# A graph network on one core: three groups of edge types asked for ahead of three bases and W1, and the maxima, scales and base splits at later slots

## The reference, cut to what matters

```python
# x: 1250 x 512, 40000 edges (src, dst sorted, type of 32, weight), bases: 8 x 512 x 512
h = relu(layernorm(x))
weight = einsum('rb,bio->rio', w_comp, bases)          # 32 relations from 8 bases
h_rel = einsum('ni,rio->rno', h, weight)
x = x + segment_sum(h_rel[type, src] * edge_weight, dst) + h_bias
h = relu(layernorm(x))
# second layer: graph convolution with self loops
u = h @ W1.T + b1
x = x + relu(segment_sum(norm[:, None] * u[row], col)) # norm = rsqrt(deg[row]) * rsqrt(deg[col])
```

## Time and profile before

| what | value |
|---|---|
| time, median of 3 runs | 731.87 us (731.0 to 733.36) |
| profiled execution, first to last instruction (its span) | 625.8 us |
| profiled execution, whole time | not given by the page |
| PE busy | 496.4 us, 79% of the span |
| DVE busy | 328.6 us, 52% |
| POOL busy | 352.2 us, 56% |
| ACT busy | 151.9 us, 24% |
| mean granted TensorE clock | 0.905 of full speed |

### The profile page before, as it was taken

How to read it: one execution, slowest core, us unless ns; L and a number is a source line. 1 busy time by engine, 2 the same in 40 slices (tenths; PEclk the granted TensorE clock), 3 DMA queues, 4 the chain that set the end, 5 groups by cost and what they waited for, 6 DMA issues and landing times.

```text
span 625.8 us, 15841 instructions
## 1 busy us (share of the span) xinstructions
PE 496.4 (79%) x5824; PEld 317.0 (51%) x5824; DVE 328.6 (52%) x929; ACT 151.9 (24%) x272; POOL 352.2 (56%) x473
## 2 busy tenths in 40 slices
PE   3031445598999899999999998999897876889996
PEld 1020334356666556666656665566564554545443
DVE  7898038885665446636655556645542221544121
ACT  3392234532222122211322202203210000341021
POOL 3334536786676776766747757677677777200000
PEclk9665657599999999999999999999997977789999
DMA  9896965557786887886858868778788788323042
GB/s 283 306 362 216 391 161 150 166 152 211 217 278 202 255 259 205 256 262 175 272 153 252 258 189 262 222 235 273 210 250 261 216 234 240 118 68 102 2 98 68
DMA packets 53427, 132.82 MB, mean 212 GB/s; under 512 B 12173, under 2 KB 18174, under 8 KB 53350
## 3 DMA queue, kind: packets, MB, share of 16 engines
q0 software_dynamic: 27040, 99.60, 53.1%
q1 hardware_dynamic: 25356, 30.99, 15.9%
q10 hardware_dynamic: 954, 1.13, 0.6%
HBM read 120.58 MB, written 11.10 MB: 210 GB/s over the span
## 4 chain that ended last, share of the span: by engine, by line
PE 52%; DMA 14%; DVE 12%; issue 8%; ACT 5%; POOL 5%; SPq 3%; ACTq 1%; POOLq 0%; DVEq 0%
PE PS L1521 22%; PE PS L1501 16%; DMA gath<-rows_layer,srcs 9%; PE PS L1595 7%; POOL gath L722 5%; PE PS L1541 4%; DMA types<-types_by_slot 2%; SPq L579 2%; DVE room_b L1225 2%; ACT room_b L841 2%; DVE zt L1225 1%; DMA edge_records<-room_c 1%; DVE room_b L1261 1%; DMA w1t<-edge_records,w1t 1%; PE PS L1507 1%
## 5 line engine op out<-in xcount | busy, mean ns | idle before, releaser
L722 POOL DMA_INDIRECT gath<-rows_layer,srcs x335 | 335.7, 1002 | 165.1 <-issue 84.8
L1501 PE MATMUL PS<-sel,gath 128*128 128x48 f16 (+7 forms) x4020 | 299.1, 207 | 52.8 <-DMA gath<-rows_layer,srcs 21.8
L1501 PEld LDWEIGHTS PS<-sel,gath 128*128 128x128 f16 x4020 | 235.4, 103 | 163.9 <-issue 86.6
L1521 PE MATMUL PS<-room_b,zt 128*128 128x512 f16 x480 | 168.6, 392 | 1.5 <-DVE sel L1147 1.0
L1521 PE MATMUL PS<-room_b 128*128 128x512 f16 (+1 forms) x480 | 151.7, 384 | 2.0 <-DMA gath<-rows_layer,srcs 1.8
L1141 DVE TENSOR_TENSOR masks<-iota_n,dloc 128x24 bf16<-128x24 f32 (+12 forms) x92 | 17.9, 194 | 96.6 <-issue 58.8
L1507 PE MATMUL PS<-oh_ad,gath 128*128 128x30 bf16 (+7 forms) x335 | 65.1, 194 | 0.0
L782 ACT CAST val<-val_f 128x64 f16<-128x64 f32 x42 | 11.0, 262 | 201.8 <-DVE val_f L1098 196.8
L1521 PEld LDWEIGHTS PS<-room_b 128*128 128x128 f16 (+1 forms) x480 | 47.8, 105 | 16.8 <-DMA gath<-rows_layer,srcs 2.1
L1521 PEld LDWEIGHTS PS<-room_b,zt 128*128 128x128 f16 x480 | 45.2, 100 | 8.6 <-issue 2.2
L1147 DVE TENSOR_TENSOR sel<-masks,val 128x192 f32<-128x192 bf16 (+12 forms) x92 | 38.6, 420 | 0.0
(11 more groups left out here) (202 smaller groups left out, 409.9 us busy)
## 6 DMA issues: line engine op xcount, KB each, us to landing
room_b<-in_L_gnn_bases_dram SPq DMA_DIRECT2D x8, 1024.0 KB, 9.3
gath<-rows_layer,srcs POOLq DMA_INDIRECT x335
types<-types_by_slot SPq DMA_DIRECT2D x168, 16.0 KB
x_t<-x_base SPq DMA_DIRECT2D x19, 128.0 KB
u_t<-in_x_dram SPq DMA_DIRECT2D x9, 256.0 KB, 6.2
x_base<-u_t SPq DMA_DIRECT2D x9, 256.0 KB
x_layer<-x_t SPq DMA_DIRECT2D x18, 128.0 KB
u_t<-x_layer SPq DMA_DIRECT2D x18, 128.0 KB, 2.7
```

Of the source, the lines that this page charges most:

```text
L722: pool.indirect_dma_start(out=gath[:, s % UN, :], out_offset=None, in_=tab0_d[:, :], in_offset=bass.IndirectOffsetOnAxis(ap=srcs[:, s:s + ...
L1501: mm(there, gath[:, s % UN, D * t + P * f:D * t + P * (f + 1)], sel_parts[:, here, k, 0:NB * w, u], start=first and t == 0 and u == 1, sto ...
L1521: last = mm(PS[0:r, PBANK[q], :], zt[q % 2][:, t, f, b, 0:r], base_hl[:, b, u, f, :], start=(m == 0), stop=(m == NM - 1))
```

## The change

Two lists are changed. SP asks for the types of groups 3, 4 and 5 together with groups 1 and 2, ahead of bases 5 to 7, the biases and W1. In the written order, "largest" moves from step 7 to 15 and "scale" from 8 to 16, and base n is split in step 17 + 2n instead of 10 + 3n, so in 17 to 31. The squares of bases 5 to 7 and of W1 stay in steps 0 to 3. Within a step, "largest" stands behind the own column of tile 0, and in step 27 the own column of tile 1 ahead of the split of base 5.

```diff
@@ -258,12 +258,12 @@
-        SQ_SETUP, SC_AT, BS_AT, WT_AT = BEARLY, 7, 10, 38
+        SQ_SETUP, SC_AT, BS_AT, WT_AT = BEARLY, 15, 17, 38
         for r in range(NTI):
             STEPS[LAST[r]].append(("flush", r))
             STEPS[LAST[r] + (3 if r + 1 < NTI else 1)].append(("own", r))
         for n in range(NB):
-            STEPS[BS_AT + 3 * n].append(("bsplit", n))
+            STEPS[BS_AT + 2 * n].append(("bsplit", n))
@@ -593,7 +593,7 @@
-            for v in range(1, TRING):
+            for v in range(1, TRING + VEARLY):
                 load_types(v)
             for n in range(BEARLY, NB):
                 load_base(n)
@@ -625,8 +625,6 @@
             sp.wait_ge(s_tab0, 16 * (NT + 3))
             sp.dma_start(w_in, W1.rearrange("(c p) i -> p c i", p=P)).then_inc(s_win, 16)
             sp.wait_ge(s_xbase, 16 * NT)
-            for v in range(TRING, TRING + VEARLY):
-                load_types(v)
             load_x(0)
             load_x(1)
```

## The result

The changed kernel took 736.2 us (median of 20 runs), the kernel before 732.3 us in the runs beside it; the ratio of the fast runs is 1.007, 95% interval 1.0049 to 1.0091, so about +5.1 us (the medians of all runs differ by 3.9). The forecast was 737.0 us, +5.2. The sign, the size and the likeliest case hold.

The account below looks back on a forecast made before the run. PE bounds the kernel from slot 38, which hangs on the last base split. W1's landing +6.5 and DVE's order -1.3 gave +5.2 on 731.87: 737.0 us, range 733.5 to 740.5, wide range 731.5 to 741.5.

Parts of the forecast that it names:

- likeliest case: Whole kernel: slower than before, 737.0 us (+5.2), chance of being slower 0.68.
- Types and the stop at slot 7: SP's queue: types land near 62 us at the latest, PE's 13.4 us stop goes, bases go out at 59.8.
- What is late next: PE stops after slot 12, ending near 77.5 us, for flush 0 behind ACT's square of W1; about 17 us.
- T: W1's landing, when ACT's square of it starts: from 83.56 to 90.1 us (87.8 to 92.3), +6.5, with 21 gathers issued before.
- The estimate that was hung on it: DMA engines: with exactly even turns between queues, T would be about 1 us earlier and the sum 1 us less.
- The order on DVE: DVE from W1's landing T: scales at T+15.2, last split ends at T+50.3 against T+51.6, so -1.3 us.
- From the last split to slot 38: Slot 38 hangs on the last split and moves with it; slot 37 just inside, costing nothing, at most +0.5.
- From slot 38 to the end: From slot 38 on PE is the bound, so a shift of slot 38 should reach the end whole.
- gathers give way: DMA: SP's queue runs at base 5's rate, W1 lands at 78.4, below 82.7 deciding; 725.4 us, chance 0.12.
- No change: DMA bill small: fewer gathers out, T near 86, sum +1.1, 733 us; chance 0.20.
- The change doesn't act: SP stuck in a types wait, DVE still waiting at group 3; chance 0.02, within the 0.20 of no change.
- The aim without ACT's hold: Slots 7 to 15 run before W1's landing T, scales at T+6.9, 729.3 us; within the 0.12.

Follow-up runs that it names:

- e4: The changed kernel with ACT's square of W1 moved from step 3 to step 15; ratio 0.9953 to the kernel before.
- e9: The changed kernel run again, unaltered, in a group where the kernel before takes 627.9 us; ratio 1.0136 to the kernel before, +8.5 us.
- e0_before: The kernel before, unchanged, profiled on a 732 us chip as neighbour of the changed kernel's profile; ratio 0.9974, span 730.6 us.
- e3: The changed kernel with POOL held before the gather of slot 15 until W1 is squared; ratio 1.0078 to the kernel before.
- e1: The kernel before with only the types of groups 3 to 5 moved ahead of the bases, steps left; ratio 1.0083 to the kernel before.
- e5: The changed kernel with types of groups 3 to 5 asked for behind bases 5 to 7, ahead of biases and W1; ratio 0.9959 to the kernel before.
- e10: The kernel before with DVE's half of the last base split done three times, same values; ratio 1.0074 to the kernel before, +4.7 us.
- e8: The changed kernel with types of groups 3 to 5 behind bases 5 to 7, W1 ahead of biases, its square in step 15; ratio 0.9972 to the kernel before.
- e11: The same kernel as e8, run again in another group; ratio 0.9927 to the kernel before.
- e2: The kernel before with only largest, scale and splits moved to the new steps, types left behind W1; ratio 1.0032 to the kernel before.

## Why the prediction was right, and where it was not

**Types and the stop at slot 7**: right. Twenty issues take 10.29 us, 0.51 each where 0.46 was taken, so the bases go out at 60.88, not 59.8. The 13.4 us wait is gone.

**What is late next**: right, in place and nearly in size. PE stops behind slot 12 (15.9 us, "about 17" was said) because ACT's square of W1 stands ahead of the cast and flush 0. The three ACT rows at 91.72, 93.63 and 93.76 show it and e4 proves it: with the square moved, slot 13 ends 10 us earlier. Slot 12 ended at 81.0, not 77.5 (78.3 in e9); 2.2 us of that are four stops inside slots 9 and 11 of the unnamed kind told of under e0_before, which e9 doesn't have.

**T**: the direction and the causes right, the size too small. 91.72 where 90.1 (87.8 to 92.3) was taken, +7.7 against e0_before, not +6.5; and in e9 93.41, past that range, +9.9 against the 83.56 that the prediction started from. The bases went out 1.1 us later than taken, which may be part of it. POOL shows the 21 gathers; the last of them and the first that had to wait:

```profile
84.74 0.95 POOL L720 DMA_INDIRECT gath<-rows_layer,srcs  x1 [1.05 <-remote]
...
99.45 1.18 POOL L720 DMA_INDIRECT gath<-rows_layer,srcs  x1 [13.77 <-PE PS L1505]
```

The two parts of the step: without the six gathers T came 4.2 us earlier (e3), and what is left, 3.6, is the head start (e1: 87.29 - 83.99 = 3.3, with one gather more than before). They aren't separate prices, though. With the head start kept (e5, on another chip), five more gathers went with a T only 1.9 us later; 1.9 and 3.6 make 5.5, so some 2 us of the 7.7 seem to come only when both are there. The queues from 60 to 78 us, answering to the earlier trace rows:

```profile
q1 hardware_dynamic: 1722, 3.16, 49.3%
q0 software_dynamic: 837, 3.08, 48.0%
```

Between them 6.24 MB in 18 us, less than the 6.94 of before. The difference lies in the first 4 us, when the bases asked for at 60.88 had hardly begun to come: 0.94 MB against 1.52. From 64 to 78 us it is 5.36 against 5.48 MB. The same rows in e9:

```profile
q0 software_dynamic: 924, 3.42, 53.8%
q1 hardware_dynamic: 1472, 2.76, 43.6%
```

There the gathers took the larger share, the last of the 21 was issued at 79.71 and not at 84.74, and W1 came 1.7 us later. The Trainium skill (DMA: Bandwidth & Descriptors, Queues, rings and completion order) says that an engine takes turns between its queues packet by packet. The shares of 49.3 and 48.0% are even, those of e9 (43.6 and 53.8%) are not, and by the profile's count SP's queue moved twice as many packets as the gathers (1722 to 837), so these rows neither show such turns nor exclude them. The estimate that was hung on it, T 1 us earlier, did not come.

**The order on DVE**: right. Scales at T+14.8 (T+15.2 was said), last split at T+49.7 (T+50.3), in the changed kernel and again in e5 (T+14.8, T+49.7) and e9 (T+49.8), whose T differ by 7.5 us. Slot 37 lies inside the splits: 138.4 against 141.4. To the last split the shift against e0_before is 7.7 - 1.8 = 5.9 us, where 6.5 - 1.3 = 5.2 was forecast.

**From the last split to slot 38**: here a term was left out. The step said that slot 38 hangs on the last split and moves with it. It moved by 8.0, not 5.9. PE around it in the changed kernel, then in e0_before:

```profile
138.24 0.18 PE L1505 MATMUL PS<-oh_ad,gath 128*128 128x50 bf16 x1
142.38 2.72 PE L1519 MATMUL PS<-room_b,zt 128*128 128x512 f16 x6 [3.96 <-DVE sel L1145]
144.90 0.45 PE L1499 MATMUL PS<-sel,gath 128*128 128x88 f16 x3
145.13 1.06 PE L1519 MATMUL PS<-room_b,zt 128*128 128x512 f16 x2
```

```profile
136.49 1.46 PE L1521 MATMUL PS<-room_b,zt 128*128 128x512 f16 x6
138.26 0.30 PE L1501 MATMUL PS<-sel,gath 128*128 128x88 f16 x3 [0.32 <-DVE room_b L1225]
138.40 0.60 PE L1521 MATMUL PS<-room_b,zt 128*128 128x512 f16 x2
```

And the changed kernel's windows there (length, busy of PE, weight loads, DVE, ACT and POOL, PE clock, DMA share, GB/s):

```profile
138.00:140.00 2.00, 0.43 (x8) 0.18 (x4) 0.96 (x1) 1.00 (x1) 1.39 (x3) 1.00 0.61 179
140.00:142.00 2.00, 0.00 (x0) 0.00 (x0) 2.00 (x4) 0.58 (x2) 2.00 (x1) 0.74 0.76 235
142.00:144.00 2.00, 1.62 (x4) 0.59 (x5) 2.00 (x7) 1.49 (x4) 1.70 (x2) 0.50 0.52 139
```

PE finishes slot 37 three microseconds before the last split, and then stands 3.96 us for the selection of slot 38, which DVE makes behind that split. The granted clock falls while it stands, to 0.50, the 1.2 GHz level, and slot 38's matmuls run at it: six products take 2.72 us where they took 1.46, the next two pairs 1.06 each where they took 0.60. Slot 38 takes 6.4 us from 142.38, in e0_before 4.2 from 136.49: 2.1 us, all of the difference between 5.9 and 8.0. The prediction noted that slot 37 would come in just inside the last split, and cost it at "nothing, at most +0.5". e9 (3.84 us idle, 2.72 for the six) and e10 (6.24 idle, 2.72) show the same; in e8 and e11 stops of 2.88 and 3.03 us gave 1.60 and 1.92. How long the lower clock then lasts doesn't follow the length of the stop: against e0_before's 4.2, slot 38 took 1.4 us more in e10, 2.1 in the changed kernel and 2.4 in e9. e2 and e3, with the last split at 140.4 in both, end slot 38 6.1 and 6.4 us behind it, where e0_before took 5.2.

**From slot 38 to the end**: "should reach the end whole" holds in its own setting, the one that the earlier trace rows show. On chips at 628 us, e10 carries +6.1 from slot 42 on to the end. e9 carries +10.1 at slot 42 and +10.4 at slot 80, then +11.5 at slot 104 and +14.2 at slot 334, which no step explains; its profiled run was the slowest of the six, 4.6 us above their median, and in the runs it is +8.5. On the chip that timed the change the slots after 38 aren't shifted alike, which the prediction had named as a sign of being wrong: the changed kernel is 8.0 us behind e0_before at slot 38, 4.9 at slot 42, 2.8 at slot 74, and then 8.2 again at slot 334; e2 is 5.7 behind at slot 38 and 0.7 ahead at slot 90. These are single executions, and the runs of the changed kernel lie between 732.6 and 742.2 us, so how much of the 8.0 us at slot 38 makes up the measured +5.1 isn't shown.

So the number was met partly by luck. In the profiles of its own setting (e9 against the profile ahead of the prediction) the terms are: T +9.9 where +6.5 was forecast, the order -1.8 where -1.3 was, and +2.4 for the clock and the stop at slot 38, where nothing was. That puts slot 38 10.5 us later, twice the forecast. The runs beside e9 lost 8.5 us, 3 more than forecast; on the chip that was asked about, less of it arrived.

**The rivals**: *gathers give way* needed T below 82.7; it was 91.72. *No change* needed T near 86; e5 shows that with the bases in front it would have been there (85.92). *The change doesn't act* is out by the missing wait. *The aim without ACT's hold* is what e4 builds, and it gains there.

Open are: the 3.7 us on ACT before flush 0 in e2; what took back e3's saving; why e1 costs 3 us more in the runs than at slot 38; and what PE's stops of the "issue" kind are, which come with the slower stretch from 150 to 520 us on some chips.

## What to carry to other kernels

When two things end together, ask which engine's queue the second one stands in: removing the first wait here only let PE run six slots further to a flush behind ACT's square of W1, and one step's place in that written order was worth more than the three groups of loads that were moved. A load moved ahead of others is paid twice, by its own issues and transfers and by what it sets free: six gathers that could now start earlier held back W1, on which slot 38 hung. And a wait just in front of a long run of matmuls can cost more than its length, since the clock may be down when they start.

## What the runs showed of the hardware

The same kernel took 628 to 630 us in two groups and 732 to 742 in three others, and in the one pair of profiles of it slot 38 ended within 0.4 us of the same time. The difference lies behind that: 184 to 186 GB/s and 209 to 213 POOL instructions from 150 to 520 us on a 732 us chip, 229 to 234 GB/s and 264 to 271 in the profiles near 628 us. Compare the changed kernel on the slower chip, whose PE clock was hardly lower than the 0.98 of the earlier trace rows, so the clock is not the reason:

```profile
150.00:520.00 370.00, 305.21 (x3558) 188.88 (x3559) 164.84 (x475) 59.51 (x132) 202.05 (x209) 0.97 0.66 184
```

There PE's stops at the edges' matmuls come to 38.1 us of the "issue" kind; in e9 they are 17.1 us for gathers and 4.8 of "issue". I had taken one profile for the kernel's behaviour everywhere. What a shift is worth at the end can depend on the chip that times it: for this change, +5.1 us in one group and +8.5 in another.

TensorE's clock: a stop of 3.96 us right ahead of slot 38 brought the granted clock from 1.00 to 0.50 (1.2 GHz), and six 128x512 matmuls took 2.72 us where they took 1.46.
